# Attention kernel: denominators from the keys' tokens plus one, experts' additions between the fills, three places for the sums

## The reference, cut to what matters

```
h = layernorm(x)                                  # tokens, mean 0 over the 128 values
f = h @ W1[:128];  g = h @ W1[128:]               # 16 values a token
scores[i, j] = tanh(f[i] + g[j] + b1) @ w2 + b2
e = exp(scores) * (j < i)
x = x + (e / (e.sum(j) + 1e-10)) @ h
p = softmax(layernorm(x) @ router_w + router_b)   # 8 experts, the best two, gates sum to 1
x = x + sum over those two of gate * (layernorm(x) @ expert_w + expert_b)
```

## Time and profile before

| | us |
|---|---|
| median of three runs | 8727.63 |
| profiled execution, own time | 8722.61 |
| its span | 8720.8 |
| ScalarE busy in the span | 5509.9 |
| VectorE busy in the span | 6552.1 |
| TensorE busy in the span | 6813.0 |
| the stage, span time 4316 to 8600 | 4284 |

### The profile page before, as it was taken

The page is one execution under the profiler, slowest core; times in us unless marked ns, Lnnn a source line. Parts: engine busy times, 40 slices in busy tenths (PEclk is TensorE's granted clock), DMA queues, the critical chain, the costliest instruction groups (busy, mean ns, idle before and its releaser), DMA issues. The chain is left out here.

```text
span 8720.8 us, 102626 instructions
## 1 busy us (share of the span) xinstructions
PE 6813.0 (78%) x37518; PEld 2473.6 (28%) x37518; DVE 6552.1 (75%) x11973; ACT 5509.9 (63%) x4244; POOL 1760.8 (20%) x1554
## 2 busy tenths in 40 slices
PE   8999999987887159957776766777777777777776
PEld 3333333323443123323322212222222222222222
DVE  6777777776764643347788887899978999889986
ACT  3222223214554342234599998999989999898995
POOL 5665566630000300005500000000000000000002
PEclk9999999987887579978999999999999999899998
DMA  1000000001010000000000000000000000000000
GB/s 47 1 1 1 1 1 1 1 4 27 23 25 6 7 0 0 0 0 3 8 1 1 1 1 1 1 1 1 10 1 1 1 1 10 1 1 1 1 10 13
DMA packets 24159, 46.19 MB, mean 5 GB/s; under 512 B 10394, under 2 KB 13596, under 8 KB 22558
## 3 DMA queue, kind: packets, MB, share of 16 engines
q1 hardware_dynamic: 23710, 40.17, 1.5%
HBM read 14.98 MB, written 8.39 MB: 3 GB/s over the span
## 5 line engine op out<-in xcount | busy, mean ns | idle before, releaser
L2437 ACT ACTIVATE aa_tanh<-aa_tanh 128x4096 f32<-128x4096 f32 (+8 forms) x1280 | 3695.9, 2954 | 291.9 <-DVE aa_tanh L2619 291.2
L2619 DVE TENSOR_SCALAR aa_tanh<-aa_f_times,aa_g_bias 128x1024 f32<-128x1024 f32 (+18 forms) x5120 | 2943.4, 646 | 458.6 <-PE aa_scores L2481 454.1
L2481 PE MATMUL aa_scores<-aa_tanh,aa_w_spread 128*32 128x512 f32 (+8 forms) x18432 | 2184.2, 592 | 852.2 <-ACT aa_tanh L2437 850.2
L2481 PEld LDWEIGHTS aa_scores<-aa_tanh,aa_w_spread 128*32 128x32 f32 x18432 | 616.2, 113 | 2253.5 <-ACT aa_tanh L2437 1198.7
L278 POOL TENSOR_TENSOR near_tap_weights<-near_hat_y_mask,near_hat_x 128x1024 f32<-128x1024 f32 x400 | 937.6, 2366 | 470.0 <-PE near_weights_spread L570 461.3
L584 PE MATMUL near_out_sum<-near_weighted,near_w_out 128*128 128x512 f32 x1984 | 994.6, 624 | 26.8 <-DVE near_weighted L357 13.5
L570 PE MATMUL near_weights_spread<-near_tap_weights,near_spread_consts 36*64 36x512 f32 x6272 | 799.7, 610 | 18.5 <-DVE near_weighted L357 13.0
L2495 PE MATMUL aa_out_sum<-aa_weights,aa_normed 128*128 128x512 f32 (+3 forms) x1152 | 611.7, 654 | 220.5 <-DVE aa_weights L2626 220.0
L346 DVE TENSOR_TENSOR near_weighted<-near_weights_spread,near_values 128x1024 f32<-128x1024 f32 x496 | 589.5, 1220 | 147.2 <-PE near_weights_spread L570 147.2
L346 DVE TENSOR_TENSOR near_weights_spread<-near_weights_spread,near_values 128x1024 f32<-128x1024 f32 x288 | 354.0, 1229 | 337.6 <-PE near_weights_spread L570 337.6
L2402 POOL TENSOR_SCALAR aa_group_normed<-x_rows,norm_scale,aa_shift_plus 128x128 f32<-128x128 f32 x96 | 79.0, 836 | 2488.2 <-PE aa_turned L2528 1767.9
(11 more groups left out here) (372 smaller groups left out, 7389.5 us busy)
## 6 DMA issues: line engine op xcount, KB each, us to landing
l_taps<-l_scan_in_out SPq DMA_DIRECT2D x256, 64.0 KB, 2.0
x_rows<-in_x SPq DMA_DIRECT2D x4, 2048.0 KB, 14.7
out_x<-x_rows SPq DMA_DIRECT2D x4, 2048.0 KB, 6.3
qa_x<-in_L_attn_w SPq DMA_DIRECT2D x1, 1024.0 KB, 5.6
L_ffn_expert_w<-in_L_ffn_expert_w SPq DMA_DIRECT2D x2, 512.0 KB
near_spread_consts<-in_deform_consts SPq DMA_DIRECT2D x1, 805.5 KB, 8.1
aa_weights_in<-in_attention SPq DMA_DIRECT2D x1, 577.5 KB
l_weights<-in_mamba SPq DMA_DIRECT2D x1, 557.0 KB
```

What stands on the lines that cost most here:

```text
L2437: a.activation(TH[:, tt, 0:length], TH[:, tt, 0:length], ACT.Tanh).then_inc(th_ready, 1)
L2481: last = t.matmul(sp_[32 * q:32 * q + 32, n % 2, s:e], W2S[:, tt, :], TH[:, tt, o + s:o + e], start=tt == 0, stop=tt == 3, tile_position=( ...
L2619: last = v.tensor_scalar(TH[:, tt, at[q]:at[q] + w - s], FR[:, m % 2, lo + s:CHUNK], GB[:, key:key + 1], None, ALU.add)
```

## The change

**Denominators.** The keys' normed tokens (`UN`) are stored with 1 added to every value. A token has mean 0, so the sum over keys of weight times token, averaged over the 128 values, is the denominator. `add_out` takes that average with bn_stats from the turned sum, inverts it, and takes the added part out again through a vector `MD`. `add_denominators`, the `den` job and `invert` are gone; only the mask stays (`mask`). `keep_turned` subtracts the 1 for the queries.

**Experts.** `add_expert(E, q)` puts one of the four dependent additions behind each of the four additions of a fill. It stands in the fill that is one step later: job s is taken during fill s+5.

**Places.** `TH` has three places in place of four: fill k waits for the scores of step k-3.

```
-PREPARE, TURN = ("turn0", "turn1", "f0", "f1", "g"), ("den", "out0", "out1")
+PREPARE, TURN = ("turn0", "turn1", "f0", "f1", "g"), ("out0", "out1")
+PLACES = 3
-        TH = sb("tanh", [P, 4, 4 * CHUNK])
+        TH = sb("tanh", [P, PLACES, 4 * CHUNK])
...
+        added = {(n + 1 + (tt == 3), (tt + 1) % 4): x[1] for (n, tt), x in behind.items() if x[0] == "e"}
...
-                    last = pool.tensor_scalar(UN[:, at:at + P], T[:, t * P:(t + 1) * P], N.scale[:, t:t + 1], N.shift[:, t:t + 1], ALU.mult, ALU.add)
+                    last = pool.tensor_scalar(UN[:, at:at + P], T[:, t * P:(t + 1) * P], N.scale[:, t:t + 1], SHA[:, t:t + 1], ALU.mult, ALU.add)
...
-                v.tensor_copy(UT[:, h * BANK:(h + 1) * BANK], bank(name, m)).then_inc(free(name, m)[0], 1)
+                v.tensor_scalar(UT[:, h * BANK:(h + 1) * BANK], bank(name, m), 1.0, None, ALU.subtract).then_inc(free(name, m)[0], 1)
...
-            def fill(n, tt):
+            def fill(n, tt, E):
-                if n:
-                    v.wait_ge(th_used, 1 + 4 * (n - 1) + tt + 1)
+                if 4 * n + tt >= PLACES:
+                    v.wait_ge(th_used, 1 + 4 * n + tt - PLACES + 1)
                 for q in range(4):
                     s = 32 * q * diagonal
                     key = 16 * j + 4 * q + tt
-                    last = v.tensor_scalar(TH[:, tt, at[q]:at[q] + w - s], FR[:, m % 2, lo + s:CHUNK], GB[:, key:key + 1], None, ALU.add)
-                last.then_inc(sum_ready, 1)
+                    ins = v.tensor_scalar(TH[:, (4 * n + tt) % PLACES, at[q]:at[q] + w - s], FR[:, m % 2, lo + s:CHUNK], GB[:, key:key + 1], None, ALU.add)
+                    if q == 3:
+                        ins.then_inc(sum_ready, 1)
+                    if E is not None:
+                        add_expert(E, q)
...
-                if j:
-                    v.tensor_tensor(DEN[:, lo:CHUNK], DEN[:, lo:CHUNK], ET[:, n % 2, 0:w], ALU.add).then_inc(den_added, 1)
...
             def add_out(m, h):
+                for k in range(4):
+                    last = v.bn_stats(ST4[:, 6 * k:6 * k + 6], bank(name, m)[:, k * P:(k + 1) * P])
+                out_ch(last)
+                st = ST4[:, :].rearrange("p (t s) -> p t s", s=6)
+                out_ch(v.tensor_tensor(D2[:, :], st[:, :, 1], st[:, :, 4], ALU.add))
+                out_ch(v.tensor_scalar(RD[:, :], D2[:, :], 0.5, 1e-10, ALU.mult, ALU.add))
+                out_ch(v.reciprocal(RD[:, :], RD[:, :]))
+                out_ch(v.scalar_tensor_tensor(MD[:, :], D2[:, :], -0.5, RD[:, :], ALU.mult, ALU.mult))
+                for k in range(4):
+                    last = v.tensor_scalar(T[:, at[k]:at[k] + P], T[:, at[k]:at[k] + P], MD[:, k:k + 1], None, ALU.add)
+                out_ch(last)
...
-                    fill(n, tt)
+                    fill(n, tt, added.get((n, tt)))
                     if n >= 2 and tt == 2:
-                        add_denominators(n - 2)
+                        mask(n - 2)
```

More of the change, by code:

```diff
@@ L2323, in own_job @@
             if m:
[L2324 removed]
+                name = {(2, 0): "out0", (2, 2): "out1"}.get((i, tt))
             if m + 1 < NM and name is None:
@@ L2396, in normalize_group @@
                 if G % NGI == 0:
-                    pool.wait_ge(sh_ready, 1 + G // NGI + 1)
+                    pool.wait_ge(sh_ready, 1 + G // NGI + 2)
                 if G:
@@ L2480, in scores @@
                         o = at[q] - 32 * q * diagonal
-                        last = t.matmul(sp_[32 * q:32 * q + 32, n % 2, s:e], W2S[:, tt, :], TH[:, tt, o + s:o + e], start=tt == 0, stop=tt == 3, tile_position=(0, 32 * q))
+                        last = t.matmul(sp_[32 * q:32 * q + 32, n % 2, s:e], W2S[:, tt, :], TH[:, (4 * n + tt) % PLACES, o + s:o + e], start=tt == 0, stop=tt == 3, tile_position=(0, 32 * q))
                 last.then_inc(th_used, 1)
@@ L2496, in add_tile @@
                 last.then_inc(o_done, 1)
[L2498 to L2503, removed]
             def turn_out(m, h):
@@ L2639, in keep_out @@
                 v.tensor_copy(OT[:, :], op[:, :]).then_inc(ot_ready, 1)
[L2641 to L2645, removed]
             def add_out(m, h):
                 name = f"out{h}"
-                v.wait_ge(rd_step, 1 + m + 1)
+                t0 = m * CT_ + 4 * h
+                at = [(t0 + k) * P for k in range(4)]
                 v.wait_ge(*full(name, m))
-                t0 = m * CT_ + 4 * h
                 for k in range(4):
-                    at = (t0 + k) * P
-                    last = v.scalar_tensor_tensor(T[:, at:at + P], bank(name, m)[:, k * P:(k + 1) * P], RD[:, 4 * h + k:4 * h + k + 1], T[:, at:at + P], ALU.mult, ALU.add)
+                    last = v.bn_stats(ST4[:, 6 * k:6 * k + 6], bank(name, m)[:, k * P:(k + 1) * P])
[9 more added lines that the diff above has]
+                for k in range(4):
+                    last = v.scalar_tensor_tensor(T[:, at[k]:at[k] + P], bank(name, m)[:, k * P:(k + 1) * P], RD[:, k:k + 1], T[:, at[k]:at[k] + P], ALU.mult, ALU.add)
                 last.then_inc(free(name, m)[0], 1)
@@ L2657, in add_out @@
                 for k in range(4):
-                    last = v.bn_stats(N.stats[:, (t0 + k) * 6:(t0 + k + 1) * 6], T[:, (t0 + k) * P:(t0 + k + 1) * P])
+                    last = v.bn_stats(N.stats[:, (t0 + k) * 6:(t0 + k + 1) * 6], T[:, at[k]:at[k] + P])
                 last.then_inc(st_ready, 1)
@@ L2718, in gating, with add_expert @@
                     gate_ch(v.tensor_tensor(GT_[:, G % 2, :].rearrange("p (t e) -> p t e", e=EX), s13, s23, ALU.add))
[L2720 removed]
+            def add_expert(E, e):
                 G, k, h = E // 8, E % 8 // 2, E % 2
                 x = T[:, (4 * G + k) * P:(4 * G + k + 1) * P]
[L2724 to L2733 removed]
+                if e == 0:
+                    v.wait_ge(*full("e", E))
+                    if h:
+                        v.wait_ge(*free("e", E - 1))
+                else:
+                    v.wait_ge(sum_step, 1 + 3 * E + e)
+                c = k * EX + 4 * h + e
+                v.scalar_tensor_tensor(x, bank("e", E)[:, e * P:(e + 1) * P], GT_[:, G % 2, c:c + 1], x, ALU.mult, ALU.add).then_inc(sum_step if e < 3 else free("e", E)[0], 1)
             def keep_back(G):
@@ L2800, in _ @@
                         v.tensor_scalar(SH1[:, :], N.shift[:, b * NT:(b + 1) * NT], 1.0, None, ALU.add).then_inc(sh_ready, 1)
-            add_denominators(len(tiles) - 2)
-            add_denominators(len(tiles) - 1)
+            mask(len(tiles) - 2)
+            mask(len(tiles) - 1)
             keep_out(NM - 1)
-            invert(NM - 1)
             for h in range(2):
```

63 lines of the change are left out of this document (17 added, 46 removed).

## The result

| | us |
|---|---|
| before, median | 8726.15 |
| after, median of four runs (9608.05 to 9619.42) | 9612.16 |
| forecast | 9180 (8890 to 9460) |
| after, span of the profiled execution | 9606.3 |

The ratio is 1.1016, 95% interval 1.0997 to 1.1035. The direction was right; the time lies outside the range.

A forecast was written before the change was run, and what follows sets the result against it. ScalarE was taken as the bound, busy 3952.0 of the stage's 4284 us. The terms summed to 507 us, less a tenth +455, so from 8722.6 us to 9180 us, 5.2% slower; range 8890 to 9460.

The forecast's parts named there:

- job's turn: TensorE's job waits for additions in a fill that needs the scores just before it: 138 turns, +327 us.
- gates: ScalarE's waits for the experts' gates, which VectorE computes behind a fill that now starts later: +20 us on 38.9.
- the idleness taken back: ScalarE's idleness already present in windows with experts' work, not to be lost twice: -80 us.
- TensorE's clock: TensorE idles more and falls to 1.2 GHz more often: +70 us, a fifth of 373.
- mask's turn: `add_tile` waits for a mask behind fill (n, 2): +40 us in experts' stretches, +60 elsewhere, bounds 0 and +200.
- fewer places against narrow tiles: Behind narrow tiles one short tanh of ScalarE's stock is lost with the place: +35 us.
- denominators and `add_out`: VectorE's work on denominators goes, -30 us; the longer `add_out` between two fills makes ScalarE late, +65 us.
- less a tenth: Taken off the sum of 507 us because several delays fall on the same steps: +455 us left.
- cushion: Time from a fill's end until its tanh is due on ScalarE: 2.3 us with three places, 5.8 with four.
- The rival built like that rule: TensorE's clock falls for good in the experts' stretches, +373 us in place of +70: 9450 us, chance 0.12.
- The two stalls a chunk: Fills late behind the two halves of the longer `add_out`, by 1.6 and 3.1 us: 16 x 4.7, taken as +65.
- The rival of relief: The job's bank is free in time, and less VectorE work cuts ScalarE's waits by some 120 us: 8600 us, chance 0.06.

The follow-up runs named there:

- both turns mended: The changed kernel, three places, with the experts' additions inside fill s+4 and the mask ahead of fill (n, 2): 8884.58 us, ratio 1.0186.

## Why the prediction was wrong

The terms of its sum against the runs. Each measured term is the difference between two neighbours on one way from the kernel before to the changed one, so they add up to the whole whatever the order; the shares depend on it:

| term | predicted | measured | from |
|---|---|---|---|
| job's turn, at the upper clock, with gates, less the idleness taken back | 327 + 20 - 80 = 267 | 286 | 461 - 175, if all of the 175 lie in the job's turns |
| TensorE's clock | 70 | at least 175 | products of zeros, in two thirds of the job's turns |
| mask's turn | 100 | 291 (in the changed kernel 261 or 267) | 9175.6 - 8884.6 |
| fewer places against narrow tiles | 35 | 161 (with both turns mended 240) | 8884.6 - 8723.2 |
| denominators and `add_out` | -30 + 65 = 35 | 7, within the noise of two runs each | 9182.7 - 9175.6 |
| additions between a fill's | in the first row | -32 | 9151.1 - 9182.7 |
| sum | 507, less a tenth: 455 | 888 | 9612.2 - 8723.2 = 889 |

*Right: the term that decides the sign.* Three places and the later fill together make TensorE stand behind its own scores: +430 us with three places, -33 with four. The number of turns (138 against 133 waits) held. Their price at the upper clock held roughly: 100 of the waits stand right between the full scores of one step and those of the next, and the 33 of these turns with scores and job at that clock last 6.0 us on average, where I had 7.3 for full fills and 6.2 for narrower ones.

*Failed: "With full neighbours the next fill is late by about 0.2 us" of the masks.* This is the step that failed. I had seen the chain and priced it in the best state: the upper clock, full neighbours, and ScalarE a full cushion ahead. The wait itself came out as I had it (3.06 us is the median of the 128, for 2.7 and 0.29), and so did the 0.2 us where I had looked: in the kernel with three places alone, at the 17 masks with full neighbours (the two tiles behind the mask's) and both scores and products at the upper clock, the tanh behind the next fill is late by 0.3 us on average. At the other 51 with full neighbours one of the two is slow, and it is late by 1.9. At the 60 with a narrow neighbour the four tanh beside it are late by 3.9 in sum, 2.6 more than in the kernel before, where I had 1 to 2. The piece above (scores of 3.31 us, products of 2.54, and 3.00 us late) is of the second kind. 291 us is also outside the bounds I gave (0 to +200). The 457.0 us of waits for masks, against 220.0, are its mark.

*Failed in size: the clock.* I took a fifth of the 373 us that it could cost; products in the job's turns alone gave back 175. In 67 of the 100 turns read above scores or job are slow, and those turns last 8.0 us, against 6.0. That the clock lengthens the mask's turn too is what the slow rows show; no run measured it apart. The Trainium skill, TensorE: Matmul & The Clock Gate, "HAM oscillation", says that short bursts between waits each begin at the slow clock; in the rows above the job and its scores do, but 33 of the 100 turns and the stage's clock of 0.85 say that others do not. The rival built like that rule, with 9450 us, was nearer to the time, but not for its reason: the whole 373 us on the clock are not borne out, and the masks and the lost place, which it left at 100 and 35 us, made up the rest.

*Failed: the tenth taken off and the 80 us taken back.* The two chains add (466 and 461 us; 267 and 261), so these two were not paid once for both. That the experts' stretches would give idleness back no run measured apart; the 461 us, where 267 + 70 = 337 had been forecast, show no sign of it.

*Failed in size: narrow tiles, gates, the other way `add_out`.* 161 us of cushion against 35, or 240 where the turns are mended. ScalarE's waits for gates went from 38.9 us to 91.6, 53 more in place of 20; what time they cost is inside the 461 and 161 us. `add_out` grew by bn_stats of 282 ns and additions of 282 ns, as estimated, but the whole new form of the denominators costs at most some 7 us with three places and gains 27 with four. The two stalls a chunk that I had for it do not show.

```profile
L2631 DVE BATCH_NORM_STATS2 aa_sums_stats<-aa_turned 128x6 f32<-128x128 f32 x128 | 28.2, 282 | 0.7 <-PE aa_turned L2504 0.7
L2639 DVE TENSOR_SCALAR x_rows<-x_rows,aa_minus_part 128x128 f32<-128x128 f32 x128 | 28.0, 282 | 1.1
```

The rival of relief holds where its condition, a bank that is free in time, does: with four places this change is 61 us faster than before, 27 by the denominators and 33 by the interleaving.

## What to carry to other kernels

Before taking a buffer from a ring, list every instruction that waits for something queued behind a fill: each moves one step closer to the step it depends on. If it then stands behind its own releaser, two engines take turns, and the price is the sum of their times, not the larger. Price such a turn in the common state, with slow products and a spent cushion, and not in the best one; and move a small step that others wait for (a mask) ahead of the large one that waits (a fill).

## What the runs showed of the hardware

Four dependent additions of 128x128 last 1.50 us in a row. Between a fill's four additions a pair starts every 0.92 us (5936.28 to 5937.20 in the changed kernel's timeline), so a fill with them takes 3.7 us where fill and additions apart take 2.7 + 1.5 = 4.2:

```profile
5936.54 0.74 DVE L2609 TENSOR_SCALAR aa_tanh<-aa_f_times,aa_g_bias 128x1024 f32<-128x1024 f32 x1
5937.20 0.34 DVE L2719 SCALAR_TENSOR_TENSOR x_rows<-aa_turned,aa_gates,x_rows 128x128 f32<-128x128 f32 x1
```

So an addition costs 0.12 us less where an independent operation stands between it and the one it depends on, with a semaphore in both cases. The Trainium skill, VectorE: DVE Perf Modes, "The DRAIN you can't avoid", has eight copies that take the same time with a semaphore after each and after the last alone. No run here leaves a semaphore out, so that stays untested; what the prediction drew from it, no gain from interleaving and 4.2 us for such a fill, the 3.7 us contradict. And bn_stats of 128x128 takes 282 ns from PSUM (the group above), as the 281 ns from SBUF in the earlier trace rows.

More work on an engine can shorten a kernel: products of zeros in TensorE's waits brought 175 us.
